# Two experts' gates in one broadcast transfer: four transfers of 512 KB per pass in place of eight of 256 KB

## The chip, the cores and the metric

The kernel runs on one core of a Trainium2 chip. Its engines work side by side, each on its own list of instructions: TensorE (PE in the profile, with its weight loads as PEld), VectorE (DVE), ScalarE (ACT), GpSimd (POOL) and SyncE (SP), which here only issues DMA transfers. They wait for each other through semaphores. The metric is the device time of one execution in microseconds; lower is better.

## The reference

The input is 16 batch rows of 512 tokens by 256 features. Each goes through a feed-forward block with half weight, windowed attention, and the same feed-forward block again:

```python
x = x + 0.5 * ffn(layernorm(x))
x = x + attn(layernorm(x))          # 16 heads of 16, window of 64 tokens
x = x + 0.5 * ffn(layernorm(x))

def ffn(X):                          # 8 experts, the best 2 of each token, and a shared one
    shared = silu(X @ sW1 + sb1) @ sW2 + sb2
    activation = sqrt(softplus(X @ routing_W.T + expert_bias))
    top_vals, top_idx = top_k(activation, 2)
    combine = sum(one_hot(top_idx, 8) * top_vals[..., None], axis=-2)
    y = silu(X @ rW1[e] + rb1[e]) @ rW2[e] + rb2[e]      # for each expert e, hidden size 128
    return shared + sum_e combine[:, e] * y[e]
```

All experts are computed for all tokens. The gate of an expert, one number per token (mostly zero), is multiplied into its hidden layer.

## The kernel before

A batch row passes three stages: p (the first feed-forward block), attention, and q (the second feed-forward block). The stages of neighbouring rows are interleaved: while row b is in attention, row b+1 is in p and row b-1 in q. The order of each engine's steps is written out by hand in tables: `HEAD` for the start, `ORDER` for the loop (`pH3-4` is step pH3 of row i-4), and `TAIL` for the end. One loop handles one row of each stage. A pass is one p or one q of one row; `nth(s, b)` numbers them.

All products are made of three matmuls, high and low parts of 32-bit numbers (`three`, lines 1071 to 1075). In a pass, the steps are, with e from 0 (the shared expert) to 8:

- TensorE `H`e: hidden layer, into one of three PSUM banks `gb`, taken in turn. The third user of a bank later waits for the one that had it before (`take_bank`), for an H step until VectorE's step `a`e has read it.
- ScalarE `t`e: tanh (line 798). VectorE `a`e: (hidden + bias) times the gate (line 1014; without a gate for e = 0, line 1007), then `g`e (line 1020) makes the silu of it. ScalarE `gh`e and GpSimd `gl`e (lines 783, 680) split it into high and low part, and TensorE `Y`e (lines 1073 to 1075, tile `yb`) multiplies by the second weight matrix.
- Before that come layer norm (statistics on VectorE, GpSimd, then ScalarE), logits and ranks on VectorE, and the gates: ScalarE `cr` writes an 8 x 512 block `cfrow`, SyncE `G1` stores it to DRAM (`gates_pair`, 16 KB), and SyncE `sp`m (line 560) reads row m of it back into all 128 partitions of `gate[:, m % 4, :]`. So `sp`m serves expert m+1, and a slot of `gate` is used twice per pass: `sp0` to `sp3` wait until the pass before has used its last four, `sp4` to `sp7` until this pass has used its first four, both by the count `f_a` of VectorE's `a` steps. `a`e waits for the semaphore `f_gate` of its slot. In the first p and the last q pass TensorE and ScalarE make the gates instead (line 790).

Attention writes keys and queries to DRAM and reads them back in another layout: per half of the heads, `QW` (lines 568 and 570, four transfers of 256 KB, after VectorE's split `ql`, line 921), `ST`c0 and `ST`c1 (lines 582 and 587, twelve transfers each). `S` (line 1142) makes the scores of a window into `sb_`, VectorE's `mx` (line 942) the masked maximum, ScalarE's `ex` (line 736) the exponentials, GpSimd `pn` (line 663) divides, TensorE's `P` (line 1151) transposes, `U` (line 1170) multiplies by the values, `O` projects, and VectorE adds that to the row (line 930).

SyncE's own order in a loop is `qsp4` to `qsp7` of one row, `QW0`, `ST00`, `ST01`, `pG1`, `OUT`, `QW1`, `psp0` to `psp3`, `VS` (shifted values, lines 595 and 598), `ST10`, `psp4` to `psp7`, `ST11`, `qG1`, `qsp0` to `qsp3`, `LX` (the next input). A transfer that waits holds all behind it.

## Time and profile before

| | us |
|---|---|
| median of 3 runs | 1540.26 (1536.65 to 1541.98) |
| the profiled execution | 1536.15 |
| its span in the profile | 1534.4 |
| TensorE busy in the span | 1498.8 |
| VectorE, ScalarE, GpSimd busy | 1158.8, 1131.7, 802.3 |

The span runs from the first to the last instruction of the program. Starts in the rows are microseconds from its beginning. The head (weights, first passes) ends near 158 us, then come 13 loops to 1424 us, then the tail. "Idle before" is the time that an engine had nothing to do before an instruction, and "<-" names what ended it. The DMA engines carry 30 passes of gates: 240 transfers of 256 KB.

### The profile page before, as it was taken

The numbers are of one execution on the slowest core, as the hardware profiler recorded it, in microseconds if no ns is written. First come the engines' busy times: TensorE is split into PE (matmuls) and PEld (weight loads), VectorE is DVE, ScalarE is ACT, GpSimd is POOL, SyncE is SP. The second block draws the span as 40 slices with busy tenths as digits, with TensorE's granted clock in tenths as the row PEclk, the third lists the DMA queues.
The fourth block names the chain that finished last, engine by engine and source line by source line (L and its number), as shares of the span: only waits on it lengthen the run. The fifth ranks groups of instructions, "written<-read, shape, count | busy, mean of one in ns | idle before, by whom it ended". The sixth has DMA issues, their size and how long they took to land.

```text
span 1534.4 us, 41376 instructions
## 1 busy us (share of the span) xinstructions
PE 1498.8 (98%) x13953; PEld 1352.9 (88%) x13953; DVE 1158.8 (76%) x4773; ACT 1131.7 (74%) x3416; POOL 802.3 (52%) x794
## 2 busy tenths in 40 slices
PE   8999999999999999999999999999999999999898
PEld 7888889888998989899898988989898898989787
DVE  6767777868788786877868788786877878686664
ACT  5477787778777877777778677777877878677754
POOL 4445555546455554645546465554655556454443
PEclk9999999999999999999999999999999999999899
DMA  4175537264363735536363454726436362534410
GB/s 120 36 188 153 151 108 193 82 184 128 98 173 110 189 98 161 138 100 184 95 177 119 126 136 122 192 81 192 120 98 172 117 182 84 153 104 136 121 56 28
DMA packets 264392, 199.66 MB, mean 130 GB/s; under 512 B 150859, under 2 KB 220918, under 8 KB 264182
## 3 DMA queue, kind: packets, MB, share of 16 engines
q1 hardware_dynamic: 263972, 196.94, 45.5%
q8 instruction: 112, 1.84, 0.5%
q14 instruction: 98, 0.80, 0.2%
q0 software_dynamic: 32, 0.07, 0.0%
q10 hardware_dynamic: 178, 0.02, 0.0%
HBM read 141.86 MB, written 42.43 MB: 120 GB/s over the span
## 4 chain that ended last, share of the span: by engine, by line
PE 66%; DVE 11%; SPq 6%; issue 6%; ACT 4%; POOL 3%; DMA 3%; DVEq 0%; POOLq 0%; ACTq 0%
PE gb L1073 9%; PE gb L1075 8%; PE gb L1074 8%; PE yb L1073 7%; PE yb L1075 6%; PE yb L1074 6%; PE ptb L1151 5%; PE sb_ L1142 5%; PE cxb L1170 3%; SPq L587 3%; DMA gate<-gates_pair 2%; POOL gl L680 2%; PE gb L1192 2%; PE gb L1190 2%; SPq L582 2%
## 5 line engine op out<-in xcount | busy, mean ns | idle before, releaser
L680 POOL TENSOR_TENSOR gl<-ag,gh 128x512 fp32r<-128x512 f32 x288 | 387.5, 1351 | 306.4 <-ACT gh L783 302.6
L736 ACT ACTIVATE pr<-pr,mx 128x128 f32<-128x128 f32 x1024 | 397.1, 392 | 34.6 <-DVE mx L942 30.8
L663 POOL TENSOR_TENSOR pr<-pr,rinv 128x512 f32<-128x512 f32 x256 | 277.9, 1092 | 231.2 <-DVE rinv L950 229.9
L1073 PE MATMUL yb<-w2h,gh 128*128 128x256 f32 x1152 | 333.9, 290 | 3.5 <-POOL gl L680 3.1
L1075 PE MATMUL yb<-w2l,gh 128*128 128x256 f32 x1152 | 321.4, 279 | 0.0
L1074 PE MATMUL yb<-w2h,gl 128*128 128x256 f32 x1152 | 321.4, 279 | 0.0
L942 DVE CUSTOM_DVE_ANT_0 pr<-sb_,mask 128x128 f32<-128x128 f32 x1024 | 235.9, 285 | 72.2 <-PE ptb L1151 47.5
L798 ACT ACTIVATE tt<-gb,b1half 128x512 f32<-128x512 f32 x288 | 195.5, 680 | 119.3 <-PE gb L1075 104.9
L1073 PE MATMUL gb<-xh,w1h 128*128 128x512 f32 x576 | 241.7, 420 | 2.5 <-DVE ag L1014 2.0
L783 ACT ACTIVATE gh<-ag 128x512 fp32r<-128x512 f32 x288 | 178.7, 626 | 84.4 <-DVE ag L1020 50.8
L1014 DVE SCALAR_TENSOR_TENSOR ag<-gb,b,gate 128x512 f32<-128x512 f32 x256 | 188.6, 745 | 65.5 <-ACT tt L798 34.1
L1020 DVE SCALAR_TENSOR_TENSOR ag<-tt,ag 128x512 f32<-128x512 f32 x288 | 228.9, 803 | 3.6
L1075 PE MATMUL gb<-xl,w1h 128*128 128x512 f32 x576 | 227.6, 395 | 0.0
L1074 PE MATMUL gb<-xh,w1l 128*128 128x512 f32 x576 | 227.0, 394 | 0.0
L1073 PEld LDWEIGHTS yb<-w2h,gh 128*128 128x128 f32 x1152 | 216.5, 188 | 10.6 <-POOL gl L680 6.6
L1074 PEld LDWEIGHTS yb<-w2h,gl 128*128 128x128 f32 x1152 | 216.6, 188 | 2.5
L1075 PEld LDWEIGHTS yb<-w2l,gh 128*128 128x128 f32 x1152 | 216.1, 188 | 0.0
L736 ACT ACTIVATION_READ_ACCUMULATOR pr<-pr,mx 128x1 f32 x1024 | 194.7, 190 | 0.0
L742 ACT ACTIVATE pt<-ptb 128x512 f32<-128x512 f32 x256 | 149.8, 585 | 48.2 <-PE ptb L1151 47.8
L1142 PE MATMUL sb_<-ks,qs 128*128 128x128 f32 x1024 | 154.9, 274 | 11.5 <-DVE mx L942 7.5
L1151 PE MATMUL ptb<-ident,pr 128*128 128x128 f32 x1024 | 159.6, 279 | 1.2 <-ACT pt L742 0.7
L1142 PEld LDWEIGHTS sb_<-ks,qs 128*128 128x128 f32 x1024 | 138.1, 191 | 23.6 <-DVE mx L942 12.0
(159 smaller groups left out, 2792.3 us busy)
## 6 DMA issues: line engine op xcount, KB each, us to landing
gate<-gates_pair SPq DMA_DIRECT2D x240, 256.0 KB, 4.0
ks<-qk_dram SPq DMA_DIRECT2D x256, 128.0 KB, 2.8
qs<-qk_dram SPq DMA_DIRECT2D x512, 64.0 KB, 2.5
qk_dram<-qkh SPq DMA_DIRECT2D x64, 256.0 KB, 2.4
qk_dram<-qkl SPq DMA_DIRECT2D x64, 256.0 KB, 3.0
vb<-va SPq DMA_DIRECT2D x32, 384.0 KB, 7.4
xres<-L_attn_x_dram SPq DMA_DIRECT2D x16, 512.0 KB, 5.1
out_dram<-axn SPq DMA_DIRECT2D x16, 512.0 KB, 3.4
```

Of the source, the lines that this page charges most:

```text
L663: nc.gpsimd.tensor_tensor(pr[:, k], pr[:, k], rinv[:, k, :].unsqueeze(2).to_broadcast([P, NP, P]), ALU.mult).then_inc(a_pn, 1)
L680: nc.gpsimd.tensor_tensor(gl[:, k, :], ag[:, k, :], gh[:, k, :].bitcast(F32), ALU.subtract).then_inc(f_gl, 1)
L736: nc.scalar.activation(pr[:, k, r, :], pr[:, k, r, :], ACT.Exp, bias=mx[:, k, r:r + 1], scale=-1.0, accum_out=rsum[:, k, r:r + 1]).then_in ...
L798: nc.scalar.activation(tt[:, g % NTT, :], bank("%sH%d" % (s[0], e), b), ACT.Tanh, bias=b1half[:, e:e + 1], scale=0.5).then_inc(f_t, 1)
L942: nc.vector.tensor_tensor_reduce(out=pr[:, k, r, :], in0=sb_[:, r, :], in1=mask[:, min(j % NW, 1), :], scale=-SCALE, scalar=3e38, op0=ALU. ...
L1014: nc.vector.scalar_tensor_tensor(ag[:, k, :], hbk, b1[:, e:e + 1], gate[:, m, :], ALU.add, ALU.mult).then_inc(f_a, 1)
L1020: nc.vector.scalar_tensor_tensor(ag[:, k, :], tt[:, g % NTT, :], 1.0, ag[:, k, :], ALU.add, ALU.mult).then_inc(f_g, 1)
L1073: nc.tensor.matmul(dst, ah, bh, start=start, stop=False, **kw)
L1074: nc.tensor.matmul(dst, al, bh, start=False, stop=False, **kw)
L1075: return nc.tensor.matmul(dst, ah, bl, start=False, stop=stop, **kw)
L1142: mm = nc.tensor.matmul(sb_[:, r, :], qs[:, w // 4, r, w % 4].rearrange("p h q -> p (h q)"), ks[:, r, k0:k0 + P], start=True, stop=True)
L1151: mm = nc.tensor.transpose(ptb[:, r * P:(r + 1) * P], pr[:, k, r, :], ident[:])
```

## The change

Step `sp`m does nothing for an even m. For an odd m it transfers rows m-1 and m of the gates into two neighbouring slots at once: 1024 elements (4 KB) to each of the 128 partitions, 512 KB. It stands where the odd step stood, with the odd step's wait on `f_a`. There are two semaphores in place of four, one for each pair of slots, and `a`e waits for its pair.

```diff
-        f_gate = [sem("f_gate%d" % k) for k in range(4)]
+        f_gate = [sem("f_gate%d" % k) for k in range(2)]
...
                 elif s[1:3] == "sp":
+
                     n, m = nth(s, b), int(s[3:])
-                    if m == 0:
+                    if m == 1:
                         sp.wait_ge(f_g1, 16 * ns(s, b) + 16)
-                    wait(sp, f_a, NE * (n - 1) + m + 6 if m < 4 else NE * n + m - 2)
-                    sp.dma_start(gate[:, m % 4, :], gates[n % 2, m].partition_broadcast(P)) \
-                        .then_inc(f_gate[m % 4], 16)
+                    if m % 2 == 1:
+                        wait(sp, f_a, NE * (n - 1) + m + 6 if m < 4 else NE * n + m - 2)
+                        sp.dma_start(gate[:, m % 4 - 1:m % 4 + 1, :], gates[n % 2, m - 1:m + 1].partition_broadcast(P)) \
+                            .then_inc(f_gate[m % 4 // 2], 16)
...
-                            dve.wait_ge(f_gate[m], 32 * ns(s, b) + 16 * ((e - 1) // 4) + 16)
+                            dve.wait_ge(f_gate[m // 2], 32 * ns(s, b) + 16 * ((e - 1) // 4) + 16)
```

Line numbers after the place grow by 2: 560 becomes 562, 1014 becomes 1016. The order of the other engines is the same, only SyncE's list changes. In a loop, SyncE has before, from `QW1` on (`VS` is the pair 595, 598, `ST10` what follows it):

```order
L570 DMA qk_dram<-qkl 128x512
L560 DMA gate<-gates_pair 128x512 [waits f_a,f_g1]
L560 DMA gate<-gates_pair 128x512 [waits f_a] x3
L595 DMA vb<-va 64x2x768 [waits a_pv,a_vl]
L598 DMA vb<-va 64x2x768
L582 DMA ks<-qk_dram 32x4x256 [waits a_s,a_qw1]
L582 DMA ks<-qk_dram 32x4x256 x3
L587 DMA qs<-qk_dram 16x16x64 x8
L560 DMA gate<-gates_pair 128x512 [waits f_a] x4
```

And now:

```order
L572 DMA qk_dram<-qkl 128x512
L562 DMA gate<-gates_pair 128x1024 [waits f_a,f_g1]
L562 DMA gate<-gates_pair 128x1024 [waits f_a]
L597 DMA vb<-va 64x2x768 [waits a_pv,a_vl]
L600 DMA vb<-va 64x2x768
L584 DMA ks<-qk_dram 32x4x256 [waits a_s,a_qw1]
L584 DMA ks<-qk_dram 32x4x256 x3
L589 DMA qs<-qk_dram 16x16x64 x8
L562 DMA gate<-gates_pair 128x1024 [waits f_a] x2
```

The groups of four have become groups of two, in the same places. In the head, in pass p2 (the third row's first block), the steps are not neighbours. SyncE had `psp3` and `psp4`, then `ST00` and `ST01` of row 1, then `psp5`:

```order
L560 DMA gate<-gates_pair 128x512 [waits f_a] x2
L582 DMA ks<-qk_dram 32x4x256 [waits a_s,a_qw0]
L582 DMA ks<-qk_dram 32x4x256 x3
L587 DMA qs<-qk_dram 16x16x64 x8
L582 DMA ks<-qk_dram 32x4x256 [waits a_s]
L582 DMA ks<-qk_dram 32x4x256 x3
L587 DMA qs<-qk_dram 16x16x64 x8
L560 DMA gate<-gates_pair 128x512 [waits f_a]
```

And now `psp3` carries experts 3 and 4, and experts 5 and 6 both come with `psp5`:

```order
L562 DMA gate<-gates_pair 128x1024 [waits f_a]
L584 DMA ks<-qk_dram 32x4x256 [waits a_s,a_qw0]
L584 DMA ks<-qk_dram 32x4x256 x3
L589 DMA qs<-qk_dram 16x16x64 x8
L584 DMA ks<-qk_dram 32x4x256 [waits a_s]
L584 DMA ks<-qk_dram 32x4x256 x3
L589 DMA qs<-qk_dram 16x16x64 x8
L562 DMA gate<-gates_pair 128x1024 [waits f_a]
```

Expert 5's gate has moved behind the 24 loads of keys and queries. In the tail, the same happens to expert 7's gate of the last p pass, which moves behind the twelve loads of `ST11` of row 14.

## Rows read from the trace of the kernel before

**Rows 1.** The page, first part: busy time of TensorE and its share.
```profile
PE 1498.8 (98%) x13953; PEld 1352.9 (88%) x13953; DVE 1158.8 (76%) x4773; ACT 1131.7 (74%) x3416; POOL 802.3 (52%) x794
```

**Rows 2.** Sums by loop: stretch and length, busy by engine, PEclk, DMA share, GB/s.
```profile
426.10:516.80 90.70, 89.97 (x855) 81.59 (x854) 71.00 (x298) 69.47 (x214) 49.52 (x48) 1.00 0.50 138
...
698.40:790.30 91.90, 90.78 (x855) 81.81 (x854) 71.21 (x298) 69.46 (x214) 49.44 (x48) 1.00 0.50 139
790.30:881.10 90.80, 90.07 (x854) 81.49 (x853) 70.94 (x297) 69.47 (x213) 49.45 (x48) 1.00 0.49 134
881.10:973.00 91.90, 90.78 (x854) 81.81 (x853) 71.20 (x297) 69.45 (x213) 49.45 (x48) 1.00 0.49 140
```

**Rows 3.** Timeline of VectorE, the p pass's first gate product: start, us, idle before.
```profile
430.15 0.72 DVE L1014 SCALAR_TENSOR_TENSOR ag<-gb,b,gate 128x512 f32<-128x512 f32 x1
...
521.17 0.75 DVE L1014 SCALAR_TENSOR_TENSOR ag<-gb,b,gate 128x512 f32<-128x512 f32 x1 [0.26 <-issue]
...
704.05 0.75 DVE L1014 SCALAR_TENSOR_TENSOR ag<-gb,b,gate 128x512 f32<-128x512 f32 x1 [1.55 <-DMA gate<-gates_pair]
...
795.06 0.75 DVE L1014 SCALAR_TENSOR_TENSOR ag<-gb,b,gate 128x512 f32<-128x512 f32 x1 [0.65 <-DMA gate<-gates_pair]
...
886.81 0.75 DVE L1014 SCALAR_TENSOR_TENSOR ag<-gb,b,gate 128x512 f32<-128x512 f32 x1 [1.55 <-DMA gate<-gates_pair]
...
1161.43 0.75 DVE L1014 SCALAR_TENSOR_TENSOR ag<-gb,b,gate 128x512 f32<-128x512 f32 x1 [2.06 <-DMA gate<-gates_pair]
```

**Rows 4.** Timeline of TensorE in the loop from 881.1 us.
```profile
887.62 0.50 PE L1073 MATMUL gb<-xh,w1h 128*128 128x512 f32 x1 [0.17 <-DVE ag L1014]
```

**Rows 5.** Waits, by total: waiter <- releaser: us, times, longest.
```profile
DVE ag L1014 <- DMA gate<-gates_pair: 12.1, 10, 2.1
```

**Rows 6.** Line 560, landings of the issues at 789.1 (four), 789.7, 736.7 and 516.5.
```profile
DMA to landing us min/median/max: 5.8/6.2/7.1
...
DMA to landing us min/median/max: 5.9/5.9/5.9
...
DMA to landing us min/median/max: 3.3/3.3/3.3
...
DMA to landing us min/median/max: 6.0/6.0/6.0
```

**Rows 7.** Timeline of SyncE's queue in the loop from 790.3 us.
```profile
791.96 0.62 SPq L598 DMA_DIRECT2D vb<-va  x1
793.40 4.04 SPq L582 DMA_DIRECT2D ks<-qk_dram  x4
```

**Rows 8.** Line 560's landing at 803.8 us, and VectorE's fifth gate product.
```profile
DMA to landing us min/median/max: 4.0/4.0/4.0
...
808.09 0.75 DVE L1014 SCALAR_TENSOR_TENSOR ag<-gb,b,gate 128x512 f32<-128x512 f32 x1
```

**Rows 9.** Pass p2: SyncE's issue, its landing, VectorE's timeline, TensorE's.
```profile
157.46 0.60 SPq L560 DMA_DIRECT2D gate<-gates_pair  x1
...
DMA to landing us min/median/max: 4.2/4.2/4.2
...
158.54 0.74 DVE L1014 SCALAR_TENSOR_TENSOR ag<-gb,b,gate 128x512 f32<-128x512 f32 x1
...
160.05 0.08 DVE L942 DVE_READ_ACCUMULATOR2_ANT mx<- 128x1 f32 x1
...
161.37 0.56 PE L1142 MATMUL sb_<-ks,qs 128*128 128x128 f32 x4
```

**Rows 10.** Pass p15: SyncE's issue of expert 8's gate, VectorE's product of expert 7.
```profile
1361.46 0.60 SPq L560 DMA_DIRECT2D gate<-gates_pair  x1
...
1363.71 0.75 DVE L1014 SCALAR_TENSOR_TENSOR ag<-gb,b,gate 128x512 f32<-128x512 f32 x1 [1.40 <-ACT tt L798]
```

**Rows 11.** Pass p1: VectorE's products of experts 7 and 8, and TensorE behind them.
```profile
103.07 1.41 DVE L1014 SCALAR_TENSOR_TENSOR ag<-gb,b,gate 128x512 f32<-128x512 f32 x2 [1.22 <-DMA gate<-gates_pair]
...
103.97 0.63 PE L1180 MATMUL gb<-ident,xn 128*128 128x128 f32 x4 [0.47 <-DVE ag L1014]
```

## The prediction, made before the changed kernel ran

> **What bounds the kernel now.** I read the views in this order: the busy shares, the sums by loop, the first gate use of each loop on VectorE, TensorE at that place, then the transfers and the issuing queue. TensorE is busy 98% of the span [rows 1], so a change pays or costs only where TensorE comes to wait, or stops waiting. The middle of the program is 13 loops of 90 to 92 us, one per batch row. The sums by loop show two kinds: loops of 90.7 to 90.8 us and loops of 91.9 us, all at a granted clock of 1.00 and with the same count of matmuls [rows 2]. What differs is the first product with a gate on VectorE (line 1014, expert 1 of the first feed-forward pass). Where it found its gate landed (430.15), its loop took 90.7 us; where it waited 0.65 us for the transfer, 90.8 us; where it waited 1.55 us, 91.9 us, twice [rows 2, 3]. TensorE shows the same place: hidden layer 3 takes the PSUM bank of hidden layer 1 and so waits for that product (0.17 us shown, behind the modelled end of the matmuls) [rows 4]. So the first 0.55 us of lateness of that gate is free, and each further microsecond costs about one: (91.9 - 90.8) / (1.55 - 0.55) = 1.1. The program waits 12.1 us, 10 times, on VectorE for gates [rows 5]; nine of the ten are this product in nine of the 13 loops (up to 2.06 us, at 1161.43 [rows 3]), the tenth is in the head [rows 11].
>
> **Four transfers instead of eight: the later landing.** Four gates issued from 789.1 us land 5.8 us (the first) to 7.1 us (the last) after their issue; the second, issued at 789.7, takes 5.9 us and so lands at 795.6, 0.7 us after the first (794.9) [rows 6]. The bytes stream one gate after the other, and the start is shared. A pair is the bytes of both, so it should land where the second gate lands now: expert 1's gate comes **0.7 us later**, expert 2's no later. Bounds: 0 (if this stretch cost by the packet, since a pair could have as many rows as one gate, each twice as long) and 1.7 us (in the loop at 516 us the first gate landed in time and the second at 516.5 + 6.0 = 522.5, 1.3 us after the first product's start at 521.17 [rows 3, 6]; its lag behind the first gate is at most 1.7). I take 0.7, the case that I read most often.
>
> Nine loops already wait at that place; each gets 0.7 us more of wait, and nearly all of it is past the free 0.55: 9 x 0.7 = 6.3, less 0.3 for the loop that waits only 0.3 us now. The four quiet loops: the one at 516 us becomes 1.3 us late and pays 1.3 - 0.55 = 0.8; another, 0.7 late, pays 0.2; two pay nothing. **Middle: +7.0 us.** The delay repeats in each loop, since the next loop's start on SyncE's queue (a key split on VectorE) moves with TensorE.
>
> The gates of experts 5 to 8 are issued from 803.8 us, twelve issues of key and query loads behind 793.40 [rows 7, 8]; the pair for 5 and 6 lands at 803.8 + 4.0 + 0.7 = 808.5, and its product starts at 808.09 [rows 8]. That is 0.4 us late, but a loop that has just lost 0.7 us at the first gate needs it 0.7 us later: nothing. In the q passes the first gate took 3.3 us [rows 6] and stood 2 us before its use, and the second four over 10 us: nothing.
>
> **The even gate's issue moves to the odd gate's place.** In the steady loops these are neighbours. At five places they are not. Gates 2 and 3 of p2 and of p12, and 6 and 7 of p14, have 5 us or more in hand or land no later than today's odd gate: nothing. In the head, the pair of experts 5 and 6 of p2 goes out at 157.46, behind 24 key and query loads, and lands 4.2 + 0.7 us later, at 162.4; the product for expert 5 runs at 158.54 now, so it is 3.8 us late [rows 9]. Behind it on VectorE stands the masked maximum of window 2, which ends at 160.1, and TensorE's next score product, at 161.37, waits for that. Slack 1.3 us, so 3.8 - 1.3 = **+2.5 us**. The bounds are 0 (made good in that loop) and 3.8. In the tail, expert 7's gate of p15 goes out at 1361.46 with expert 8's, 3.3 us plus 0.7 to landing, 1365.5, against a product at 1363.71 [rows 10]: 1.8 us late, less the 0.7 of this loop and the free 0.55: **+0.5 us**. In p1 the gates of experts 7 and 8 are waited for already, 1.22 us, with TensorE waiting 0.47 behind them [rows 11]: 0.7 more, **+0.6 us**.
>
> **What it saves.** 120 issues of about 0.45 us on SyncE's queue. In the loop the two saved before the key and query loads let those be reached 0.9 us earlier, but they start at 793.40, once the rows that they read have landed, 0.8 us after the queue was through with 791.96 [rows 7]. The q gates stand before `QW0`, which waits for VectorE's key split and so sets the queue's next start. The second saving lets expert 5's pair wait for nothing else. TensorE is behind none of these issues: 0, at best 0.5 us in a few loops.
>
> Sum: 7.0 + 2.5 + 0.5 + 0.6 = 10.6, say **+10 us**. The profiled execution took 1536.15 us (span 1534.40), 4.1 us less than the median 1540.26 of runs that spread over 5.3 us. On its own time the sum gives 1546, on the median 1550; I take **1549 us**.
>
> **A page on this.** The landing rows show four transfers of 256 KB 0.7 us apart, with their fixed part shared [rows 6]. The Trainium skill, "DMA: Bandwidth & Descriptors", section "Rules for kernel authors", says to coalesce many small transfers into one large one, and its section "Anatomy of one DMA" fits a transfer as about 2.0 us plus its bytes at 436 GB/s. By that slope the second half of a pair is an estimated 0.6 us, which would make the middle about 6 us in place of 7; by the coalescing rule read alone, the change should gain. The trace does not agree with the latter: the fixed part was overlapped already, so nothing is there to save.
>
> **Rivals.**
> 1. *The halved packets pass the slow start faster* (not slower). The first gate of a p pass needs 5.8 us where a q pass needs 3.3 [rows 6]; it queues behind 1 MB of writes of keys and queries. If the 2.5 us between are a price per packet, a pair of 4 KB rows lands with today's first gate, or before it. It decides where the pair lands 1.0 us before today's first gate (4.8 us after the issue where rows 6 have 5.8), since that brings a wait of 1.55 to the free 0.55: then the excess of the slow loops goes, 3 loops of 1.1 us and up to 3 us in the last three, -6 us, and the head's +3 remains: 1540.3 - 3 = 1537. Against it: the second gate follows the first at 0.7 us, so by then the engines run by the byte.
> 2. *The later gate is hidden.* The free 0.55 us were larger, or the loops that wait now were held by something that comes with the wait. Then only the head pays, 0 to 4 us: 1542. For it: TensorE shows only 0.17 us of idle there [rows 4]. Against: the sums by loop.
> 3. *Dearer.* A pair lags 1.3 to 1.7 us behind today's first gate in the loops, as at 516 us, with the second pair late too: 13 x 1.2 + 4 = 20, so 1560.
> 4. *The descriptors stay 2 KB, 256 of them.* Then the bytes stream alike and the time is the forecast's.
>
> **How the numbers follow.** Forecast (with rival 4) 0.60, +6 to +14; hidden 0.22, 0 to +5; dearer 0.09, +14 to +22; halved packets 0.09, -8 to +1. A measurement of this kernel tells 0.3% (4.6 us) from no change. Slower: 0.60 x 0.93 + 0.22 x 0.1 + 0.09 = 0.67. Faster: 0.09 x 0.4 and a little for chance = 0.05. Same: the rest, 0.28. The range that leaves out some of the first rival and the top of the third: 1539 to 1559.
>
> **What would show it.** 120 gate transfers of 512 KB, with a median to landing near 4.7 us where it is 4.0 now. VectorE's wait for gates up from 12.1 to about 26 us, in 13 or more places: 2.2 us in the loops at 698 and 881 (now 1.55), 1.3 in the one at 790. Loops of 92.6 and 91.5 us in place of 91.9 and 90.8. A wait of nearly 4 us near 158.5 and a TensorE gap near 161. If the waits grow and the loops do not, rival 2 holds; if the first gate's wait shrinks, rival 1. If TensorE's extra idle stands elsewhere than behind line 1014 and the GpSimd split, the account is wrong.

## Result and profile after

The changed kernel takes 1558.04 us (median of four runs, 1557.22 to 1562.37) beside 1540.36 us of the kernel before on the same chip (four runs now, 1536.65 to 1541.98): a ratio of 1.0131, 95% interval 1.0112 to 1.0151, or +17.7 us. The direction was forecast, the time is inside the range at its upper end, and the change of the time is twice what was forecast (+9 us).

The page of the changed kernel, its rows on TensorE, on the gate product (line 1016 now) and on the gate transfers; then two rows of its waits by total (us, times, longest).

```profile
PE 1513.2 (97%) x13953; PEld 1362.2 (87%) x13953; DVE 1158.1 (74%) x4773; ACT 1133.2 (73%) x3416; POOL 801.6 (51%) x794
...
L1016 DVE SCALAR_TENSOR_TENSOR ag<-gb,b,gate 128x512 f32<-128x512 f32 x256 | 188.7, 746 | 89.9 <-DMA gate<-gates_pair 40.7
...
gate<-gates_pair SPq DMA_DIRECT2D x120, 512.0 KB, 4.6
```

```profile
DVE ag L1016 <- DMA gate<-gates_pair: 40.7, 23, 5.7
...
PE gb L1075 <- DVE ag L1016: 10.3, 4, 3.6
```

There are 120 transfers of 512 KB with a median landing of 4.6 us, as forecast (4.7). VectorE waits 40.7 us for gates where it waited 12.1 [rows 5] and where 26 was forecast, 23 times in place of 10. TensorE now shows waits behind the gate product of up to 3.6 us, where [rows 4] had 0.17 and the longest of the kernel before was 1.25 (at 1162.23 us, in p13).

To see where the time went, cut the program into four stretches at VectorE's first `xres` product of a batch row, as [rows 2] do for single loops: the head (here up to 243.8 us, so with the loop that begins at 158; the 13 loops follow it), the ten middle loops (gates of p3 to p12), the last three loops (p13 to p15) and the end. Sums by stretch, first of the kernel before, then of the changed one; the columns are those of [rows 2], the third from the end being the granted clock.

```profile
0.00:243.77 243.77, 230.27 (x2019) 206.49 (x2020) 175.50 (x700) 167.94 (x486) 116.32 (x134) 0.99 0.46 129
243.77:1153.94 910.17, 902.05 (x8522) 816.52 (x8521) 710.62 (x2971) 694.65 (x2122) 496.00 (x480) 1.00 0.49 137
1153.94:1424.08 270.14, 266.36 (x2526) 240.87 (x2525) 207.18 (x862) 206.21 (x635) 145.03 (x139) 1.00 0.47 136
1424.08:1534.40 110.32, 100.17 (x892) 89.02 (x890) 65.46 (x243) 62.88 (x178) 44.97 (x41) 0.95 0.21 58
```

```profile
0.00:250.14 250.14, 234.65 (x2019) 210.10 (x2020) 175.73 (x699) 168.44 (x486) 115.96 (x134) 0.97 0.44 126
250.14:1166.34 916.20, 905.60 (x8522) 817.24 (x8521) 710.14 (x2970) 695.66 (x2122) 496.08 (x480) 1.00 0.49 137
1166.34:1448.83 282.49, 271.41 (x2526) 244.48 (x2525) 206.67 (x861) 206.23 (x635) 144.56 (x139) 0.98 0.45 129
1448.83:1560.60 111.77, 101.53 (x892) 90.38 (x890) 65.57 (x243) 62.88 (x178) 45.04 (x41) 0.94 0.20 57
```

The head is 6.4 us longer, the ten loops 6.0, the last three 12.4, the end 1.4. This profiled execution is the slowest of the four runs of its kernel (1562.37 us), and the one of before (1536.15) is a little below the fastest of its runs (1536.65), so the four differences add up to 26.2 us and not to 17.7; the second profiles below take that apart. Two things are to be seen: the ten loops got 0.6 us each, about what was expected of them, the last three got 4 us each; and in the head and the last three the granted clock is lower than before.

The places themselves. VectorE's timeline of the changed kernel: the first product of the two loops that answer to 704.05 and 795.06 in [rows 3], expert 5 of p2, and the first products of p14 and p15.

```profile
713.34 0.75 DVE L1016 SCALAR_TENSOR_TENSOR ag<-gb,b,gate 128x512 f32<-128x512 f32 x1 [1.51 <-DMA gate<-gates_pair]
...
805.38 0.75 DVE L1016 SCALAR_TENSOR_TENSOR ag<-gb,b,gate 128x512 f32<-128x512 f32 x1 [1.19 <-DMA gate<-gates_pair]
...
164.02 0.75 DVE L1016 SCALAR_TENSOR_TENSOR ag<-gb,b,gate 128x512 f32<-128x512 f32 x1 [3.44 <-DMA gate<-gates_pair]
...
1269.16 0.75 DVE L1016 SCALAR_TENSOR_TENSOR ag<-gb,b,gate 128x512 f32<-128x512 f32 x1 [5.72 <-DMA gate<-gates_pair]
...
1364.82 1.41 DVE L1016 SCALAR_TENSOR_TENSOR ag<-gb,b,gate 128x512 f32<-128x512 f32 x2 [4.02 <-DMA gate<-gates_pair]
```

In the first of these two loops the wait did not grow (1.55 us before, and 2.2 was forecast), nor in the one that answers to 886.81 (1.42 for 1.55); the four loops that had not waited now do, 0.98 to 1.40 us each.

The landings (line 562) of the first pairs issued at 706.95, 1259.01 and 1358.12 us, where the first gates of the same three passes took 6.1, 4.8 and 4.2 us in the kernel before ([rows 6] had 5.8 for another loop):

```profile
DMA to landing us min/median/max: 6.3/6.3/6.3
...
DMA to landing us min/median/max: 10.0/10.0/10.0
...
DMA to landing us min/median/max: 6.6/6.6/6.6
```

And TensorE behind three of these waits, with its idle time in brackets, then sums by slice of 5 us around two of them (TensorE's busy time is the second number, the granted clock the third from the end).

```profile
164.82 0.79 PE L1075 MATMUL gb<-xh,w1h 128*128 128x512 f32 x1 [2.72 <-DVE ag L1016]
...
1269.96 0.50 PE L1075 MATMUL gb<-xh,w1h 128*128 128x512 f32 x1 [3.56 <-DVE ag L1016]
...
1365.62 0.50 PE L1075 MATMUL gb<-xh,w1h 128*128 128x512 f32 x1 [3.12 <-DVE ag L1016]
```

```profile
160.00:165.00 5.00, 2.28 (x20) 2.04 (x19) 1.56 (x6) 0.00 (x0) 0.35 (x1) 0.98 0.99 303
165.00:170.00 5.00, 5.00 (x25) 4.42 (x26) 4.30 (x19) 2.82 (x11) 1.16 (x3) 0.68 0.95 244
...
1265.00:1270.00 5.00, 1.44 (x39) 1.07 (x38) 0.81 (x2) 0.30 (x1) 0.00 (x0) 1.00 0.94 236
1270.00:1275.00 5.00, 5.00 (x17) 3.87 (x18) 4.96 (x16) 1.68 (x3) 2.50 (x4) 0.66 0.58 154
```

After each of these gaps of about 3 us TensorE works on at a granted clock of 0.66 to 0.68 over the next slice: part of it at 2.4 GHz and part at 1.2. Two matmuls of one kind in the second slice show it: the successor of the one at 1271.66 us starts 0.43 us later, at 1272.09, that of the one at 1274.21 only 0.23 us later, at 1274.44:

```profile
1271.66 0.63 PE L1077 MATMUL gb<-xl,w1h 128*128 128x512 f32 x1
...
1274.21 0.39 PE L1077 MATMUL gb<-xl,w1h 128*128 128x512 f32 x1
```

Such a slice costs an estimated 5.00 x (1 - 0.66) = 1.7 us on top of the gap. The same sum over all slices of 5 us from the start to the last stretch gives 3.4 us of lost clock in the kernel before and 11.9 in the changed one. In the last three loops the two ways of counting meet: TensorE is busy 5.05 us longer there with the same 2526 matmuls, and the sum of lost clock is 5.1; its idle time has grown by 7.3 us (from 3.8 to 11.1).

Not all of the lost clock stands behind a gap. In the changed kernel it also fell with TensorE busy throughout, as in this slice, and in the kernel before at 180 us (0.74):

```profile
1230.00:1235.00 5.00, 5.00 (x60) 4.50 (x60) 2.70 (x12) 0.21 (x1) 0.96 (x1) 0.82 0.58 213
```

Of the 11.9 us, 5.1 stand behind the three gaps above.

### The profile page after: what moved, and what is told of

It reads as the page before. It is cut to its first block, busy times and chain, and to the rows that moved or that the text cites. A ratio compares the mean times of both kernels' runs of the same rounds, so it can differ in the third digit from the quotient of the medians.

```text
span 1560.6 us, 41256 instructions
## 1 busy us (share of the span) xinstructions
PE 1513.2 (97%) x13953; PEld 1362.2 (87%) x13953; DVE 1158.1 (74%) x4773; ACT 1133.2 (73%) x3416; POOL 801.6 (51%) x794
## 4 chain that ended last, share of the span: by engine, by line
PE 49%; SPq 13%; DVE 12%; DMA 9%; issue 7%; POOL 5%; ACT 4%; DVEq 0%; POOLq 0%; ACTq 0%
SPq L589 7%; DMA gate<-gates_pair 6%; PE gb L1075 6%; PE yb L1075 6%; PE gb L1077 5%; PE gb L1076 5%; PE yb L1077 5%; PE yb L1076 5%; PE ptb L1153 4%; SPq L584 3%; PE sb_ L1144 3%; PE cxb L1172 2%; POOL gl L682 2%; DMA qk_dram<-qkl 2%; PE gb L1194 2%
## 5 line engine op out<-in xcount | busy, mean ns | idle before, releaser
L1075 PE MATMUL gb<-xh,w1h 128*128 128x512 f32 x576 | 245.2, 426 | 11.0 <-DVE ag L1016 10.3
L1016 DVE SCALAR_TENSOR_TENSOR ag<-gb,b,gate 128x512 f32<-128x512 f32 x256 | 188.7, 746 | 89.9 <-DMA gate<-gates_pair 40.7
L1144 PE MATMUL sb_<-ks,qs 128*128 128x128 f32 x1024 | 156.5, 276 | 12.3 <-DVE mx L944 8.7
```

Of the source, the lines that this page charges most:

```text
L1016: nc.vector.scalar_tensor_tensor(ag[:, k, :], hbk, b1[:, e:e + 1], gate[:, m, :], ALU.add, ALU.mult).then_inc(f_a, 1)
L1075: nc.tensor.matmul(dst, ah, bh, start=start, stop=False, **kw)
L1144: mm = nc.tensor.matmul(sb_[:, r, :], qs[:, w // 4, r, w % 4].rearrange("p h q -> p (h q)"), ks[:, r, k0:k0 + P], start=True, stop=True)
```

## Experiments

All numbers in one table; the words follow below it. Ratios are to the kernel before, run on the same chip. Stretches are us of one profiled execution, cut as above; "clock" is the sum of 5 us x (1 - granted clock) over the first three stretches.

| kernel | median us | ratio, 95% interval | head | ten | three | end | clock |
|---|---|---|---|---|---|---|---|
| before | 1540.3 | | 243.8 | 910.2 | 270.1 | 110.3 | 3.4 |
| b_again | 1537.6 | 0.9999, 0.9982 to 1.0016 | 245.0 | 909.9 | 271.9 | 108.0 | 6.8 |
| changed | 1558.0 | 1.0131, 1.0112 to 1.0151 | 250.1 | 916.2 | 282.5 | 111.8 | 11.9 |
| a2_again | 1556.7 | 1.0125, 1.0103 to 1.0147 | 250.4 | 916.9 | 280.5 | 108.2 | 10.2 |
| e1_place | 1541.1 | 1.0022, 1.0009 to 1.0035 | 249.3 | 911.0 | 272.2 | 111.1 | 8.6 |
| e2_even | 1557.0 | 1.0123, 1.0103 to 1.0142 | 248.3 | 917.6 | 278.1 | 110.4 | 6.8 |
| e5_rows | 1555.9 | 1.0120, 1.0101 to 1.0139 | 247.0 | 922.3 | 274.2 | 110.7 | 5.1 |
| e3_first_only | 1545.3 | 1.0052, 1.0036 to 1.0069 | 243.7 | 915.6 | 276.0 | 108.0 | 5.1 |
| e4_first_single | 1547.4 | 1.0070, 1.0053 to 1.0087 | 249.5 | 913.5 | 274.3 | 108.2 | 8.6 |
| e8_both | 1553.1 | 1.0106, 1.0082 to 1.0131 | 252.7 | 918.7 | 272.5 | 108.2 | 8.5 |
| e6_first | 1535.4 | 0.9995, 0.9984 to 1.0007 | 245.4 | 907.3 | 270.4 | 110.9 | 5.1 |
| e9_best | 1537.9 | 0.9996, 0.9980 to 1.0012 | 244.8 | 907.7 | 276.2 | 110.8 | 8.6 |
| e11_tail_vs | 1548.4 | 1.0072, 1.0046 to 1.0098 | 247.7 | 917.3 | 272.0 | 107.8 | 5.1 |
| e12_ahead | 1541.8 | 1.0032, 1.0017 to 1.0046 | 247.8 | 909.7 | 274.4 | 111.0 | 6.8 |
| e10_hold | 1590.0 | 1.0334, 1.0296 to 1.0372 | 252.2 | 947.4 | 277.7 | 111.4 | 18.7 |
| e13_hold_tail | 1558.7 | 1.0142, 1.0115 to 1.0168 | 249.9 | 917.1 | 283.0 | 111.0 | 10.3 |
| e14_hold_all | 1568.0 | 1.0193, 1.0167 to 1.0219 | 247.5 | 936.3 | 280.1 | 111.8 | 15.4 |

### How far a stretch can be trusted: both kernels again

No edit in either: the kernel before and the changed one, profiled a second time.

> The kernel before, unaltered, profiled a second time, for the spread of head, middle and tail from one execution to the next (243.8, 910.2 and 380.5 us in the first): 1 to 3 us each if the differences of the stages between kernels are to be read as such; more, and only differences of medians count.

> The changed kernel unaltered, for a second profile. The first profile has 26 us more span than the kernel before, where the medians differ by 17.7; 12 us of the 26 lie in the loops of rows 13 to 15 (waits of 5.7, 4.0 and 4.0 us for a gate pair, landings of 10.0 and 6.6 us). Theory A (these waits belong to the change: pairs behind the value shift VS, and the moved place): they come again, and the ratio is 1.013. Theory B (that execution was a bad draw for the tail): they are under 3 us here, and the middle loops alone show +0.6 us each as before.

The two profiles of before agree within 0.3 us in the ten loops and within 1.8 us in the head and the last three; the end is 108 or 110 to 112 us in all kernels of the table, whatever was edited, and is left out of every argument. Against the mean of the two (244.4, 910.0, 271.0) the change costs +5.7 and +6.0 us in the head, +6.2 and +6.9 in the ten loops, +11.5 and +9.5 in the last three. The long waits in the last three came again (5.7 us at p15 in the second profile), so they belong to the kernel. Of the 10.2 us of lost clock in the second profile 6.8 stand behind waits for a gate (p2, p13 and p15); the rest, 3.4 us there and 6.8 in the first, is no more than what the two profiles of before have (3.4 and 6.8).

### The place of the issue alone, and the pair at the other place

e1_place keeps eight transfers and moves the even gate's issue behind the odd one's wait:

```
-                    if m == 0:
+                    if m == 1:
                         sp.wait_ge(f_g1, 16 * ns(s, b) + 16)
-                    wait(sp, f_a, NE * (n - 1) + m + 6 if m < 4 else NE * n + m - 2)
-                    sp.dma_start(gate[:, m % 4, :], gates[n % 2, m].partition_broadcast(P)) \
-                        .then_inc(f_gate[m % 4], 16)
+                    if m % 2 == 1:
+                        wait(sp, f_a, NE * (n - 1) + m + 6 if m < 4 else NE * n + m - 2)
+                        for j in (m - 1, m):
+                            sp.dma_start(gate[:, j % 4, :], gates[n % 2, j].partition_broadcast(P)) \
+                                .then_inc(f_gate[j % 4], 16)
```

> Eight single transfers of 256 KB with a semaphore each, as before, but the even gate is issued at the odd gate's place, with the odd gate's wait, right ahead of it. In the steady loops that is the order of before. Place theory: what the change costs beyond the middle loops comes from here: pass p2 waits 3.5 us for the gate of expert 5 (TensorE loses 2.7), the last p pass 2 to 4 us for that of expert 7, so the ratio to before is 1.004 to 1.006 (+6 to +9 us). Size theory (the pair as one transfer is the cause, head and tail too): at most +3 us, ratio 1.002.

e2_even sends the pair, but at the even gate's place in the order:

```
-                    if m % 2 == 1:
-                        wait(sp, f_a, NE * (n - 1) + m + 6 if m < 4 else NE * n + m - 2)
+                    if m % 2 == 0:
+                        wait(sp, f_a, NE * (n - 1) + m + 7 if m < 4 else NE * n + m - 1)
```

> Pairs as in the change, but issued at the even gate's place (with the odd gate's wait). Place theory: the head's 2.7 us and the wait for expert 7's gate in the last p pass go; +6 us in the middle loops remain, and the tail's first-gate waits; ratio to before 1.006 to 1.009. Size theory: ratio 1.010 to 1.013, as the change.

The place alone costs 0.22% (+3.4 us), and the table shows all of it in the head, +4.9 us (an estimated 2.5 of it lost clock): the product for expert 5 of p2 waits 2.53 us for its gate, with gate 5 going out behind 24 key and query loads. The ten loops are at 911.0. With the pair at the other place the cost stays at 1.23%. So the size of the transfer, not its place, is the bulk. e2_even's head is still +3.9 us, though VectorE finds the gate of expert 5 of p2 landed. There the pair stands ahead of the 24 key and query loads and holds them back: it waits for `f_a` until 144.17 us, so that the loads start at 144.59 where they start at 140.38 in the kernel before, and TensorE waits for the last of them; the slice of 155 to 160 us behind that gap is at 0.66.

```profile
154.30 0.66 PE L1144 MATMUL sb_<-ks,qs 128*128 128x128 f32 x4 [2.70 <-DMA qs<-qk_dram]
```

### The packets

e5_rows leaves padding between the gate rows in DRAM (576 numbers to a row in place of 512), so that the pair goes as 256 pieces of 2 KB and not as 128 of 4 KB.

```
-        gates = nc.dram_tensor("gates_pair", (2, E, L), F32, kind="Internal").ap()
+        gates = nc.dram_tensor("gates_pair", (2, E, L + 64), F32, kind="Internal").ap()[:, :, 0:L]
```

> The change with padded rows in DRAM (576 numbers instead of 512), so that a pair cannot be read as one 4 KB row and goes as two rows of 2 KB: the same bytes in twice the packets. Byte theory: no difference from the change (within 2 us; first gate landing about 6.1 us in p passes). Packet theory (4 KB packets start or share badly, which makes the landings of 8 to 11 us): the long landings shrink to under 7 us and the time falls by 3 to 8 us. If the halved packets had been a help, it is slower than the change by 2 us or more.

The pages' rows of all packets, of the changed kernel and of this one, show that the edit does what it says: 15,360 more, 128 for each of the 120 transfers.

```profile
DMA packets 247112, 199.66 MB, mean 128 GB/s; under 512 B 148939, under 2 KB 218998, under 8 KB 246902
```

```profile
DMA packets 262472, 199.66 MB, mean 128 GB/s; under 512 B 148939, under 2 KB 218998, under 8 KB 262262
```

1.0120 beside 1.0125: in the sum the size of the packets does not matter. The long landings did not go either: 17 of the 120 took over 7 us, 15 and 16 in the two profiles of the change. The stretches are less alike: its head and last three loops are shorter than the change's (247.0 and 274.2), where its first pairs of p13 to p15 landed in 6.5, 5.1 and 5.7 us. One profile can't say whether the packets have a part in that. Its ten loops are the longest of the group (922.3), and they show something else. Two of its waits there are about 3 us (3.11 at 345.46 and 2.98 at 899.32), and behind these two alone the granted clock drops in a middle loop. VectorE, TensorE and the slices at the first and the slice at the second:

```profile
345.46 0.75 DVE L1016 SCALAR_TENSOR_TENSOR ag<-gb,b,gate 128x512 f32<-128x512 f32 x1 [3.11 <-DMA gate<-gates_pair]
...
346.26 0.50 PE L1075 MATMUL gb<-xh,w1h 128*128 128x512 f32 x1 [1.73 <-DVE ag L1016]
```

```profile
340.00:345.00 5.00, 4.53 (x32) 4.00 (x31) 1.08 (x11) 4.21 (x17) 2.08 (x2) 1.00 0.93 235
345.00:350.00 5.00, 3.74 (x41) 2.76 (x42) 4.46 (x14) 1.32 (x2) 1.28 (x1) 0.77 1.13 221
...
900.00:905.00 5.00, 4.88 (x43) 3.57 (x44) 4.92 (x15) 1.32 (x2) 2.34 (x4) 0.66 1.08 220
```

In the changed kernel, where the waits at the first product of the ten loops are 0.9 to 1.5 us, and in e8_both, where waits of 2.34 and 2.87 us left TensorE idle for 0.96 and 1.49 us, no slice of the ten loops is below 1.00.

That a gap takes the clock down is not certain from its length alone. Take every gap of TensorE behind a gate product in all 17 profiles, from 60 us to the end of the last three loops: of 16 between 0.9 and 1.4 us none was followed by a lower clock, of 23 between 1.4 and 2.0 seven were, of 11 between 2.0 and 2.5 eight, and of 22 from 2.5 us on 19. This is one of the other three, expert 5 of p2 in e11_tail_vs (below); the slice of 165 to 170 us behind it is at 1.00:

```profile
163.39 0.50 PE L1075 MATMUL gb<-xh,w1h 128*128 128x512 f32 x1 [2.94 <-DVE ag L1016]
```

### Which pair

e3_first_only sends gates 1 and 2 as a pair and 3 to 8 alone; e4_first_single does the reverse (`PAIRS = (2, 4, 6)`). Each transfer has a semaphore of its own.

```
+        PAIRS = (0,)
...
+                    if m - m % 2 not in PAIRS:
+                        wait(sp, f_a, NE * (n - 1) + m + 6 if m < 4 else NE * n + m - 2)
+                        sp.dma_start(gate[:, m % 4, :], gates[n % 2, m].partition_broadcast(P)) \
+                            .then_inc(f_gate[m], 16)
-                    if m % 2 == 1:
+                    elif m % 2 == 1:
```

> Edit: of the eight gate transfers of a pass only the first two go as one of 512 KB; gates 3 to 8 go alone, where the kernel before issues them. Size theory (a 512 KB transfer read back to all partitions lands later at the first product of a p pass, 1 to 4 us, and that wait is paid in the loop): nearly the whole of the change's cost is here, +11 to +16 us on the kernel before, 1549 to 1553 us; the loops 1 to 11 are 0.5 to 1.5 us longer than before and the last two over 3 us. Later-pairs theory (the loss is at experts 5 to 8 and in the head and the tail): 0 to +5 us, 1537 to 1542.

> Edit: the mirror image; gates 1 and 2 go alone, 3 to 8 as three pairs at the odd gate's place. Size theory at the first product: the middle loops are as before (90.7 to 91.9 us), the head and the last p pass keep what the place of the pairs 5 and 6, 7 and 8 costs (+3 to +5 us): 1541 to 1543 us. Later-pairs theory: +11 to +16 us, 1549 to 1553. If both kernels of this pair cost about half of the change, the two effects add up and neither is the seat.

Neither theory held alone: 1.0052 and 1.0070, +8.0 and +10.8 us with intervals of 2.5 us to either side, and their sum, 18.8, is the change. The first pair costs nothing in the head and +5.6 us in the ten loops and +5.0 in the last three. The later pairs cost +5.1 in the head, +3.3 in the last three and +3.5 in the ten loops, where the prediction had put nothing.

### Waiting for both gates, without one large transfer

e8_both is the kernel before with one more wait:

```
                             dve.wait_ge(f_gate[m], 32 * ns(s, b) + 16 * ((e - 1) // 4) + 16)
+                            if m % 2 == 0:
+                                dve.wait_ge(f_gate[m + 1], 32 * ns(s, b) + 16 * ((e - 1) // 4) + 16)
```

> Edit: the kernel before, eight transfers of 256 KB at their places, but VectorE's first product of a pair waits for both gates of it. If what the pair costs is only that the first product has to wait for the second gate's bytes (the reasoning of the prediction: 0.7 us later): +6 to +14 us on the kernel before, and the waits of the last two p passes as in the changed kernel (4 to 6 us). If the one large transfer is itself slower than two small ones one after the other (its landing up to 10 us): this kernel costs 2 to 8 us, clearly less than the change, and its waits at the first product stay below 3 us.

1.0106, 85% of the change (+16.3 of +19 us), with the transfers of before; its interval and the change's overlap, so that here the stretches and the waits must tell. Head and ten loops are as long as in the change or longer: there the cost is that the first product waits for the second gate's bytes, as the prediction reasoned. The last three are not: +1.5 us in place of +9.5 to 11.5. Its first product of p15 waited 2.30 us:

```profile
1362.68 1.41 DVE L1016 SCALAR_TENSOR_TENSOR ag<-gb,b,gate 128x512 f32<-128x512 f32 x2 [2.30 <-DMA gate<-gates_pair]
```

In p13 to p15 both singles of the first pair had landed 5.5 to 5.7 us after the first one's issue (4.4 to 5.8 in the two profiles of before). The pair as one transfer took 4.4, 10.0 and 6.6 us in the change and 7.4, 5.4 and 7.5 in its second profile. So in the last three loops the one large transfer is itself slower than two small ones, on average by more than a microsecond.

### The last three loops: what stands ahead of the pair, and behind

There the copy of the values (`VS`, two transfers of 384 KB) stands ahead of the gates. e11_tail_vs puts the first pair ahead of it, for p13 as shown and for p14 and p15 alike:

```
-OUT=10 pG1=13 VS=12 psp0=13 psp1=13 psp2=13
+OUT=10 pG1=13 psp0=13 psp1=13 VS=12 psp2=13
```

> Edit: the changed kernel; in the tail's order of SyncE's queue the copy of the values (VS, two transfers of 384 KB) goes out behind the first pair of gates of p13, p14 and p15, not ahead of it. Theory T (the tail's cost is that the first pair's 512 KB land behind the 768 KB of VS): the first pair of these passes lands less than 5 us after its issue (now 6.6 to 10), VectorE's waits there of 4 to 6 us fall below 2 us, and the time falls 4 to 8 us, to 1548 to 1554. Rival (the last loops are long for another reason, since waiting for both gates as singles gave waits of 2.7 and 2.3 us there and no longer tail): 0 to -2 us, 1555 to 1558.

As the theory had it: 1.0072, 8 us less than a2_again, and the last three loops are 8.5 us shorter (272.0), with the ten loops as in the change. The head is 2.6 us shorter too (247.7), though SyncE's order there is the change's: it has the wait of 3.66 us and the gap of 2.94 in p2, but no lower clock behind them. The landings of the first pairs issued at 1255.75 (p14) and 1350.02 (p15):

```profile
DMA to landing us min/median/max: 4.2/4.2/4.2
...
DMA to landing us min/median/max: 4.5/4.5/4.5
```

e10_hold and e13_hold_tail hold back what stands behind. In the first SyncE waits for the first pair's landing before it issues the second pair, in all p passes; in the second behind the second pair, in p13 to p15; e14_hold_all does as e13_hold_tail in all p passes. The edit of e13_hold_tail (e10_hold has `m == 1` in the condition, and neither it nor e14_hold_all the `b >= 13`):

```
+                    if m == 3 and s[0] == "p" and b >= 13:
+                        sp.wait_ge(f_gate[0], 32 * ns(s, b) + 16)
```

> Edit: the changed kernel; in the p passes SyncE waits after it issued the first pair of gates until that pair has landed, so that no later transfer (second pair, values, key and query loads) shares the DMA engines with it. Theory F (the first pair lands late because what follows it on the queue takes its place on some engines): the pair lands within 4.5 to 5.5 us in the loops (now 5.3 to 7.4), and the waits at the first product fall by 0.7 us or more. Rival (the pair's own bytes and what is ahead of it set the landing): the landing stays within 0.3 us of what it is now. In both, the key and query loads come 3 to 5 us later, which may cost by itself, so the total says little: 1550 to 1590.

> Edit: the changed kernel; in p13, p14 and p15 SyncE waits, behind its issue of the second pair of gates, until the first pair has landed, and only then goes on to the key and query loads (ST10). Theory F (in the tail the first pair lands late because the twelve loads that follow on the queue are issued sooner than before and take its place on some engines): the first pair of these passes lands within 5.2 us of its issue (6.6 to 10.0, or 5.4 to 7.5, in the two profiles of the change), VectorE's waits there fall to 2 to 3 us, the last three loops come to 271 to 275 us (281 to 283 in the change, 270 to 272 before), and the time falls 5 to 10 us, to 1547 to 1552. Rival (what is ahead of the pair, the copy of the values, holds it): landing 6 us and more, the loops as in the change or longer, since the loads come later: 1556 or more.

> Edit: as e13_hold_tail, but in all 15 p passes. Theory F: in the steady loops, too, the first pair lands 0.5 to 1 us sooner (5.3 to 6.3 us in the change, 4.2 to 5.3 where SyncE waited ahead of the second pair), its wait falls below 1 us; the copy of the values and the loads behind it come 1 to 3 us later. If these have the slack, the middle ten loops fall from 916 to 910 to 913 us; if not, they grow above 918 and the loads are the tighter of the two. Rival (nothing behind the pair matters): waits and loops as in the change.

The landings of the first pair: of p14 in e13_hold_tail (issued 1260.31) and in e10_hold (1293.96), and that of the loop that answers to 706.95 in e10_hold (729.05).

```profile
DMA to landing us min/median/max: 8.6/8.6/8.6
...
DMA to landing us min/median/max: 4.5/4.5/4.5
...
DMA to landing us min/median/max: 4.4/4.4/4.4
```

My theory for e13 fell as far as the time goes: with the key and query loads held back the pair still took 6.8, 8.6 and 7.1 us, and the last three loops stayed at 283.0. In e14_hold_all, which has the same wait in these three passes, it took 4.2, 5.2 and 6.0 us, and the loops were still 280.1 us; so what the loads do to its landing stays open. With the second pair held back too it took 4.3, 4.5 and 5.0 us, although the copy of the values stood ahead as before. So the first pair is often late in the last three loops where it has 768 KB ahead of it and more gates right behind it; with either gone it landed in 4.2 to 5.0 us each time. In the ten loops what stands behind matters as well: the first pair took 4.7 us on average in e10_hold (4.0 to 5.3) where it took 6.2 and 5.9 in the two profiles of the change. But holding it back is dear: most of the ten loops grow to 92 to 98 us, 1.0334 and 1.0193. The waits move to the fifth product, 29 us in the ten loops of e10_hold, since the pair for experts 5 and 6 stands behind the loads on the held queue; TensorE waits there, and hardly more than before for the loads themselves (4.4 us for 3.2). Its waits at the place that takes the fifth product's bank, line 1180 in the kernel before, where it had waited 0.5 us, once:

```profile
PE gb L1184 <- DVE ag L1018: 29.1, 12, 4.0
```

### The wait at the first gate, taken away

e6_first is the kernel before and e12_ahead the changed one, with gates 1 and 2 issued ahead of the second half of the key and query rows in the steady loops; e12_ahead and e9_best have the edit of e11_tail_vs too.

```
-pG1-4 OUT-7 QW1-5 psp0-4 psp1-4 psp2-4
+pG1-4 OUT-7 psp0-4 psp1-4 QW1-5 psp2-4
```

> Edit: the kernel before with the issues of gates 1 and 2 of the p pass moved ahead of the second 1 MB of key and query rows written out (QW1) in the steady loops' order of SyncE's queue. Theory (the first gate of a p pass is late because it queues behind those writes): its landing falls from 5.8 us to about 3.3 us as in a q pass and its issue is no later, VectorE's 12 us of waiting for gates mostly go in the 11 steady loops, the loops of 91.9 us become 90.8 and the time falls 3 to 6 us to 1532 to 1534. Rival: the writes that start later hold up the key and query loads behind them, or the issue of QW1 was not what the gate queued behind: within 2 us of before, or slower.

> Edit: the kernel before with eight single transfers; in the steady loops gates 1 and 2 of the p pass are issued ahead of the second half of the key and query rows (as in e6_first), and in the tail gates 1 and 2 of p13 to p15 ahead of the copy of the values. Theory (a wait of VectorE at the first gate is paid in the loop, beyond a free half microsecond): the loops of p13 to p15 lose 1 to 1.5 us each, 1531 to 1534 us, 0.15 to 0.4% under before. Rival (those waits are covered in the tail): within 0.1% of before.

> Edit: the changed kernel with the first pair of gates of the p pass issued ahead of its large neighbours everywhere behind the head: ahead of the second half of the key and query rows in the steady loops, ahead of the copy of the values in the tail. Theory (the rest of the change's cost is the wait for the first pair in the middle loops, +6 to +7 us, and in the head, +3 to +6): the ten loops of the middle come back to 907 to 911 us in sum (910.2 before, 916 to 917 changed), the tail stays at 380 to 382, the head at 247 to 251, and the time is 1540 to 1544 us. Rival (the middle's cost is not that wait): the waits go, the middle stays at 914 or more, 1546 to 1550.

The waits of the three kernels, in this order:

```profile
DVE ag L1014 <- DMA gate<-gates_pair: 5.0, 6, 2.1
```

```profile
DVE ag L1014 <- DMA gate<-gates_pair: 9.8, 9, 3.5
```

```profile
DVE ag L1016 <- DMA gate<-gates_pair: 21.1, 15, 3.3
```

e12_ahead brings the ten loops to 909.7 us, beside 916 to 917 in the change and 910.0 before, and the time is 1541.81, as forecast. On the kernel before, the same order brings the ten loops to 907.3 (three loops of 91.6 to 91.9 us are now 90.7 to 90.9), but the time moves by less than can be told, 0.9995 with an interval of 0.9984 to 1.0007: the rival's size. So like beside like, both with the first gates ahead, the pairs still cost 2 us in the ten loops (909.7 beside 907.3 and 907.7), with four waits at the fifth product (3.1 us in sum): of the 6 to 7 us there, 4 to 5 are the wait for the first pair. The theory of e6_first was wrong in its mechanism: the first gate's landing did not fall towards 3.3 us, it took 5.0 us on average in the ten loops where it took 5.1. It is issued 2.5 us sooner, and that is what ends the waits; why it takes longer than in a q pass is open. The gates' move ahead of the copy of the values (e9_best) gains nothing: the waits at the first product of p13 and p14 go, 3.5 and 1.65 us come at the fifth, and the last three loops take 276.2. No version beats the kernel before by an amount that can be measured.

## Why the prediction was right and wrong

**Right: what bounds, and nearly the lag.** The first product with a gate was the place, and the wait beyond a free half microsecond was paid. In the ten loops the prediction's terms are 6 x 0.7 - 0.3 for the loops that waited and 1.0 for those that did not, +4.9; measured +6.2 and +6.9. Counted from the start of its loop, the first pair lands 1.0 us later than the first gate did (5.2 and 5.3 us beside 4.3 and 4.2, on average), where 0.7 was taken. The sum of the ten first waits rose from 5.9 to 12.3 us in the first profiles, from 5.2 to 13.0 in the second. In the mean of both profiles the six loops that had waited are 4.1 us longer (3.9 forecast) and the four quiet ones 2.4 (1.0 forecast). e8_both shows the reason (waiting for the second gate's bytes) and e12_ahead the place. The pair for experts 5 to 8, put at nothing, has a part in it too: 2 us by e12_ahead beside e9_best, 3.5 by e4_first_single.

**Right: it is the bytes.** Rival 4 was false as to the packets (4 KB, as its neighbour rival 1 assumed) and right that in the sum they do not matter; rival 1 is out, since 4 KB (the change) and 2 KB (e5_rows) give one time. Rival 2 is out by the ten loops themselves and by e12_ahead. The coalescing rule of the Trainium skill, "DMA: Bandwidth & Descriptors", section "Rules for kernel authors", read alone, does not hold here: the 120 issues and fixed parts saved gained nothing in any stretch. Its row names 64 KB as the size below which a transfer is mostly overhead, and these were of 256 KB. The fit that the prediction takes from the same page is one of transfers that GpSimd issues, and SyncE issues these; its estimate of 0.6 us for a pair's second half is below the 1.0 us measured.

**Rival 3 named the time but not the way.** The measured +17.7 us is in its band (+14 to +22, chance 0.09). It had 1.2 us for each of 13 loops and 4 for the rest; the ten loops cost 0.6 to 0.7 each, and the excess is at the two ends.

**The head: the step that was missing is the clock.** The head was forecast at +2.5 + 0.6 = +3.1 and measured at +5.7 and +6.0. The wait at expert 5 of p2 was well sized (3.44 and 4.75 us where 3.8 was forecast, at 164.02 us). The gap is 2.72 us where 2.5 was worked out, but the path was another: TensorE waits for the gate product itself, whose bank the next hidden layer takes, and not for the masked maximum behind it. In every profile with this wait the gap is 0.7 us shorter than the wait (3.44 and 2.72, 4.75 and 4.03, 2.53 and 1.81 in e1_place), so the slack was 0.7 and not 1.3, and that 2.5 came out so near is in part luck. What was missing is behind the gap: the slice at 0.68, 1.6 us more. The lost clock of the head is 6.8 us in both profiles of the change, 3.4 and 5.1 in those of before. e11_tail_vs, with the same order in the head and a gap of 2.94 us that left the clock up, has a head of +3.3.

**Wrong, and the largest: the last three loops.** They were counted as three ordinary loops, 3 x 0.7, plus 0.5 for expert 7 of p15: +2.6. Measured: +11.5 and +9.5. Three things make the difference. The pair's lag there was not 0.7 us but up to 5 (10.0 beside 4.8 in p14): the first waits of p13 to p15 were 1.7, 5.7 and 4.0 us in the change (3.0, 2.3 and 5.7 again) beside 2.1, 1.8 and 1.1 before (0.6, 2.1 and 2.2 again), 6 us more in sum, because these pairs go out right behind the copy of the values, with more gates behind them. The "0.7" was read in a steady loop, where that copy stands behind the gates. Expert 7 of p15 waited 4.1 and 3.8 us for a pair that was forecast 1.8 us late. And the clock fell behind two of the gaps in either profile, an estimated 1.7 us each; in the first it fell a third time without a gap, as in one of the profiles of before. The order of SyncE's queue in the tail was before me, and the rows for it were not read beyond the one issue at 1361.46.

**The sum, term by term.** The mean of the two profiles of the change less that of the two of before, in us:

| | head | ten loops | last three | sum |
|---|---|---|---|---|
| forecast | 3.1 | 4.9 | 2.6 | 10.6 |
| measured | 5.9 | 6.5 | 10.5 | 22.9 |
| of it lost clock | 2.6 | 0 | 3.4 | 6.0 |
| the rest | 3.3 | 6.5 | 7.1 | 16.9 |

(The sum of lost clock also counts a lower clock inside a gap, some 0.8 us in a2_again's head.) So without the clock the head was right, the ten loops were a quarter short, and the last three were mis-sized by a factor of almost three. These four executions lie further apart than the medians (22.9 us in three stretches beside 17.7 and 19 us in the whole). The mean granted clocks of all runs bear the clock's part out: 0.990 in the eight runs of the change and 0.994 in the 69 of the kernel before that were run beside the experiments, so about 16 us of lost clock beside 9 (14 beside 10 where both ran on one chip): 5 to 7 of the 18 to 19 us.

The prediction priced a wait at the wait alone, at most 1.1 us for each microsecond, which its loops bore out up to waits of 1.55 us; it had no case in which a wait is long enough to cost twice. A page tells of the two levels, though not for this kernel: the Trainium skill, "TensorE: Matmul & The Clock Gate", section "What's actually happening", has two clock states, 2.4 GHz for a busy array and 1.2 after idleness. The slices behind the 2.72 and 3.56 us gaps agree, with 0.68 and 0.66.

**What stays open.** Why 512 KB in one transfer land so late in the last three loops, in a place where the two singles of e8_both have both landed 5.5 to 5.7 us after the first's issue. The Trainium skill, "DMA: Bandwidth & Descriptors", section "Why a DMA increments its semaphore by 16 and not by 1", says that a transfer is spread over up to 16 engines and has landed only with the last of them, so that one engine that is behind holds the whole pair; no run here tells the engines apart. Open too is what makes the clock fall behind one gap and stay up behind a like one.

## What to carry to other kernels

- Putting transfers together can gain issues and fixed parts only where the queue or the first byte is waited for. Where the pieces already overlap, the first consumer waits for the bytes of all of them, at every place where it stood without slack.
- Price a wait behind TensorE in two parts: for a short gap, the gap; for a gap of 3 us, add what the lower clock most likely takes behind it (here an estimated 1.7 us, after 19 of 22 gaps of 2.5 us or more).
- A lag that is read in the steady loop holds for the neighbours on the queue that the transfer has there. Where the head or the tail has another order, read its rows by themselves; the head cost here almost as much as the ten loops, and the last three loops more.
- Compare like with like: what the pairs cost once the first gates go out sooner is seen beside the kernel with single transfers in that same order, not beside the kernel before.

## What the runs showed of the hardware

- Behind TensorE gaps of 2.5 us or more that a gate product ended, the granted clock fell to 1.2 GHz 19 times of 22 (slices of 5 us at 0.66 to 0.68 in the change), behind those of 1.4 to 2.5 us 15 times of 34, behind those of 0.9 to 1.4 us never in 16. It also fell with no gap ahead, in both kernels.
- The first pair of a p pass, 512 KB, landed in 4.7 us on average with nothing issued behind it until it had landed (e10_hold), and in 6.2 and 5.9 with the next ones right behind (two profiles of the change), in the same ten loops.
- With 768 KB ahead and more gates behind, one 512 KB transfer took 4.4 to 10.0 us in two profiles of the change, where two of 256 KB had both landed 4.4 to 5.8 us after the first one's issue (before, b_again, e8_both).
